# The late steps of a fused decoder layer: where one row update, two normalizations and the block transposes stand in VectorE's order

## The reference, cut to what matters

```
x = layernorm(x + attention1(x))                       # bf16, conv + 16 heads
x = layernorm(x + self_and_cross_attention(x, ctx))    # fp32, 16 heads, causal self part (512 keys)
                                                       # plus cross part (1024 keys), softmax over keys
x = layernorm(x + routed_ffn(x))                       # cluster and tile choice, spline; layernorm with
x = layernorm(x)                                       # gamma and beta, then a last plain layernorm
```

## Time and profile before

| | us |
|---|---|
| median of 3 runs | 2223.72 (2222.45 to 2225.03) |
| the profiled execution, its own time | 2221.05 |
| its span, first to last instruction | 2219.3 |
| PE busy | 2093.4 (94%) |
| DVE busy | 1754.5 (79%) |
| ACT busy | 1533.8 (69%) |
| POOL busy | 755.5 (34%) |

### The profile page before, as it was taken

The page is one execution under the profiler, slowest core; times in us unless marked ns, Lnnn a source line. Parts: engine busy times, 40 slices in busy tenths (PEclk is TensorE's granted clock), DMA queues, the critical chain, the costliest instruction groups (busy, mean ns, idle before and its releaser), DMA issues.

```text
span 2219.3 us, 39450 instructions
## 1 busy us (share of the span) xinstructions
PE 2093.4 (94%) x13138; PEld 911.5 (41%) x13138; DVE 1754.5 (79%) x4869; ACT 1533.8 (69%) x3361; POOL 755.5 (34%) x802
## 2 busy tenths in 40 slices
PE   5999999999999999999999999999999999989983
PEld 2344334543444434543335433454344533444332
DVE  6957779688987889778897788968888787977754
ACT  2936887478865888458894688747886578846861
POOL 3026521165113650155402653116521353004620
PEclk8899999999999999999999999999999999999995
DMA  3700034000520006100160003400043000610000
GB/s 111 138 10 1 1 67 86 11 2 1 114 49 10 2 20 124 20 11 2 39 124 10 1 1 76 87 11 1 1 96 58 11 1 11 113 30 1 1 11 10
DMA packets 250858, 81.80 MB, mean 37 GB/s; under 512 B 236064, under 2 KB 247328, under 8 KB 250656
## 3 DMA queue, kind: packets, MB, share of 16 engines
q1 hardware_dynamic: 250656, 79.29, 17.6%
HBM read 16.35 MB, written 4.19 MB: 9 GB/s over the span
## 4 chain that ended last, share of the span: by engine, by line
PE 76%; DVE 12%; ACT 8%; issue 3%; DMA 1%; SPq 0%; POOL 0%; DVEq 0%; POOLq 0%; ACTq 0%
PE bank L1738 14%; PE bank L1807 14%; PE bank L1798 10%; PE bank L1421 7%; PE bank L1734 6%; ACT work L772 5%; PE bank L1795 4%; PE bank L1691 4%; DVE work L977 3%; PE bank L1554 3%; PE bank L1541 2%; PE bank L1577 2%; PE bank L1848 2%; PE bank L1767 1%; DVE stats L982 1%
## 5 line engine op out<-in xcount | busy, mean ns | idle before, releaser
L831 ACT ACTIVATE work<-bank 128x512 f32<-128x512 f32 (+3 forms) x1536 | 723.0, 549 | 261.9 <-PE bank L1795 140.5
L1244 DVE TENSOR_REDUCE top_half<-bank 128x1 f32<-128x512 f32 x1024 | 636.4, 683 | 139.7 <-PE bank L1738 138.4
L1738 PE MATMUL bank<-k_c,q_c 32*128 32x512 f32 x2048 | 536.0, 618 | 0.0
L1798 PE MATMUL bank<-q_c,k_c 32*128 32x512 f32 x2048 | 467.4, 624 | 7.4 <-DVE q_c L1270 6.0
L772 ACT ACTIVATE work<-work,neg 128x512 bf16<-128x512 bf16 x512 | 362.7, 716 | 30.6 <-DVE work L977 29.8
L1807 PE MATMUL bank<-work,v_flat 128*32 128x512 f32 (+3 forms) x3072 | 365.0, 551 | 0.6 <-ACT work L831 0.3
L977 DVE TENSOR_SCALAR_CACHE_REDUCE work<-bank 128x512 bf16<-128x512 f32 x512 | 322.3, 685 | 35.2 <-PE bank L1523 25.1
L1241 DVE CUSTOM_DVE_ANT_0 masked<-bank,mask_w 128x384 bf16<-128x384 f32 (+3 forms) x512 | 226.6, 489 | 118.5 <-PE bank L1734 113.9
L654 POOL TENSOR_TENSOR featA<-featA,featB 128x512 f32<-128x512 f32 (+3 forms) x232 | 241.9, 1043 | 225.9 <-ACT featB L844 223.0
L1738 PEld LDWEIGHTS bank<-k_c,q_c 32*128 32x128 f32 x2048 | 210.9, 183 | 159.8 <-DVE top_half L1244 125.7
L615 POOL TENSOR_SCALAR ln_r<-mv 128x4 f32<-128x4 f32 x32 | 9.0, 281 | 748.9 <-DVE mv L986 748.9
(11 more groups left out here) (208 smaller groups left out, 2627.6 us busy)
## 6 DMA issues: line engine op xcount, KB each, us to landing
xT_pad<-xT SPq DMA_DIRECT2D x16, 256.0 KB, 2.9
ctx_sb<-ctxT SPq DMA_DIRECT2D x8, 512.0 KB, 3.4
x_res<-x SPq DMA_DIRECT2D x8, 512.0 KB, 5.0
out<-r_sb SPq DMA_DIRECT2D x8, 512.0 KB, 2.9
work<-work SPq DMA_TRANSPOSE x112, 4.5
qk_sb<-qkT SPq DMA_DIRECT2D x1, 512.0 KB, 4.6
pe_sb<-pe_w SPq DMA_DIRECT2D x1, 256.0 KB, 4.0
v_sb<-vT SPq DMA_DIRECT2D x1, 256.0 KB, 5.0
```

The source lines that it names most:

```text
L831: nc.scalar.activation(pT[:, s % PT_SLOTS, g, q0:S], exp_bank(n)[:, 0:S - q0], ACT.Exp, scale=SCALE).then_inc(pT_ready, 1)
L1244: nc.vector.tensor_reduce(top_half[:, i % 2, g, u // 2, u % 2:u % 2 + 1], scores, AX.X, ALU.max, negate=True).then_inc(slot_out, 1)
L1738: mm(dst, q_c[rows, i, P * t:P * (t + 1)], k_c[rows, i, S * half:S * (half + 1)], start=True, stop=True, tile_position=(GW * g, 0)).then_i ...
L1798: mm(dst, k_c[rows, i, P * u:P * (u + 1)], q_c[rows, i, :], start=True, stop=True, tile_position=(GW * g, 0)).then_inc(sT_mm, 1)
```

## The change

Three edits in DVE's order and one in a wait of PE:

```diff
-    QK_LATE = {LATE_STEP + 2: (0,), LATE_STEP + 4: (1,), LATE_STEP + 6: (2,), LATE_STEP + 8: (3,)}
+    QK_LATE = {LATE_STEP + 4: (0,), LATE_STEP + 5: (1,), LATE_STEP + 6: (2,), LATE_STEP + 7: (3,)}
...
                 for s in range(ALL_STEPS):
-                    if prev and s == LATE_STEP:
-                        third_sums(c, sf)
-                    if prev and s == LATE_STEP + 2:
+                    if prev and s == LATE_STEP + 4:
                         third_norm(c)
-                    if prev and s == LATE_STEP + 5:
+                    if prev and s == LATE_STEP + 6:
                         last_sums(c, sf)
-                    if prev and s == LATE_STEP + 7:
+                    if prev and s == LATE_STEP + 8:
                         last_norm(c)
...
                     for part in end_rows(s) if s >= LATE_STEP else []:
                         put_rows(*part)
+                    if prev and s == LATE_STEP:
+                        third_sums(c, sf)
...
                     if n >= FIRST_LATE + len(LATE_EXP_BANKS):
                         pe.wait_ge(pT_ready, b * ALL_SCORES + n - len(LATE_EXP_BANKS) + 1)
-                    elif n >= FIRST_LATE + 2:
-                        pe.wait_ge(slot_out, base + uses["late"])
+                    elif n >= FIRST_LATE + LATE_RING:
+                        at = LATE_EXP_BANKS[n - FIRST_LATE]
+                        pe.wait_ge(slot_out, base + max(use for use in range(uses["late"]) if use % RING == at) + 1)
```

## The result

| | before | changed |
|---|---|---|
| median of 20 runs each, us | 2224.57 (2220.91 to 2235.14) | 2215.11 (2209.24 to 2225.31) |
| ratio, 95% interval | | 0.9948 [0.9937, 0.9960] |
| profiled execution, us | 2221.05 | 2210.52 |
| mean granted clock of PE, profiled execution | 0.972 | 0.976 |

A forecast was written before the change was run, and what follows sets the result against it. PE held 76% of the chain and stopped 0.85 us at step 40 for DVE's `put_rows`. Rows first 6.4 us less POOL 0.5 gave 5.9 off 2223.72, 2217.8 us; the range for 8 in 10 was 2212.5 to 2222.3.

The forecast's parts named there:

- What bounds the kernel, and rows first: PE at step 40 waits for `put_rows` behind `third_sums`; moving it first gains 0.92 us in seven batches, 6.4 us.
- What becomes late on DVE: DVE's late steps: output copy at most 0.1 us late, at +9.4; `third_norm` from +10.0; 3.52 us to spare at the end.
- The moves of `third_norm` and of the transposes: On DVE: `third_norm` ends 4.5 us later; transposes are done by +19.8, PE needs them at about +23.8, costing nothing.
- POOL: Later convolution and rstd delay `last_norm` to +24.2, meeting the next scores: 0.1 us lost in five batches, 0.5 us.
- the lower bound: POOL term's bound of 0: the bias addition, beside which L630 took 1.80 us instead of 1.57, now comes before it.
- the control: The first batch, with no previous batch to normalize: step 40 at +4.72, next batch's first score tile at +24.21.
- Rival 1: POOL's chain through `last_norm` ends after the next batch's first scores: 0.5 us in five batches, 2219.8 us; chance 0.13.
- Behind POOL's second half: SP's loads end at +31.9, the first DMA block transpose is wanted at +32.04: fits with 0.1 us to spare.
- Bank waits: PE's transposed scores 154 and 155: 154 may start 0.62 us earlier, 155 waits as before; costed at 0.
- The clock: PE's low-clock stretch costs a batch 2.4 us; shifting batches can change how many have it, either way.
- rival 3: PE's clock turns in favour: one or two batches lose the low stretch, 2215.4 or 2213.0 us; chance 0.13.
- The sum: Whole kernel: 6.4 - 0.5 = 5.9 us off, giving 2215.1 profiled and 2217.8 for the median.

The follow-up runs named there:

- rows_behind_sums: The changed kernel with `third_sums` again ahead of `put_rows`: median 2229.88 us, 1.0015 of before.
- fill4: The changed kernel with four needless matmuls on PE ahead of step 40's transposed scores, in seven batches: median 2226.23 us, 0.9996 of before.
- transposes_as_before: The changed kernel with the four pairs of block transposes back at steps 40, 42, 44 and 46: median 2243.02 us, 1.0066 of before.
- changed_again: The changed kernel run once more, unaltered, on another occasion: median 2216.16 us, 0.9946 of before.
- no_bank_waits: The changed kernel with the old wait of PE for the banks: median 2219.37 us, 0.9971 of before.
- rows_only: The kernel before with only `put_rows` moved ahead of `third_sums`: median 2250.15 us, 1.0096 of before.
- late_bank_last_on_before: The kernel before with the new bank waits and late bank order 4, 5, 2, 3, 0, 1: median 2233.32 us, 1.0026 of before.

## Why the prediction was right, point by point

- *What bounds the kernel, and rows first.* Right. `put_rows` at +2.76 and step 40 at +4.72 in all seven batches; the first tile at +24.29 instead of +25.13, 0.84 us each. rows_behind_sums and fill4 show that this is the place that pays.
- *What becomes late on DVE.* Right to 0.1 us: the copy at +9.43 against +9.4, `third_norm` from +10.04, `finish` at +14.22, the last copy at +19.69. But that "its reader on PE comes later still" passed over how little later, 0.2 us. The moves of `third_norm` and of the transposes were costed at nothing, as if the gain didn't hang on them; the experiments show that they are what makes rows first pay at all.
- *POOL.* Half right. The term of 0.5 us is 0 as a POOL effect: `last_norm` ended at +23.7 or earlier, and not at +24.2: the chain took 9.65 us and not 10.12. Of these 0.47 us, 0.24 are L630, which the bias addition no longer met (1.56 and not 1.80), as the lower bound had it, and 0.24 are L615 (0.24 and not 0.48), which no term had. In its place stands a term that I didn't have: the first tile came 0.08 us later than the control's +24.21 in every batch, also in the seventh, where DVE was idle for 2.67 us before it. In rows_behind_sums it is 0.08 too (25.21 against 25.13). So it isn't a wait for POOL. PE's first scores (L1523) start at +23.78 in both, and DVE takes the first tile out 0.42 us later in the control and 0.51 later in the changed kernel. In all kernels run here it is 0.42 to 0.43 where a block transpose or the output copy stands just ahead of that tile on DVE, and 0.51 to 0.52 where `last_norm` does. So it comes with making `last_norm` the last thing ahead of the tile. In sum 0.08 x 6 = 0.5 us, the same as the forecast's term by accident. Rival 1 did not occur here; its mechanism is real, as transposes_as_before shows, at 1.26 us a batch.
- *Behind POOL's second half.* Right: the first block transpose by DMA went out at 570.45, +32.11, against a wanted +32.04. But the second batch gave 0.7 us back later, when PE waited 1.05 us for one such transpose (at 629.79), and its distance to the third shrank by only 0.11. The wait comes back at this place, 0.89 in changed_again and 0.97 in no_bank_waits, and was 0.42 before. "A transposed tile late by a few tenths costs nothing" is therefore not borne out in this batch; what makes the wait longer stays open.
- *Bank waits.* Right, 0, by the reason given. What was missed is the edit beside it: the wait per bank is worth 1.2 us a batch once the banks are taken in the order in which they come free.
- *The clock.* The term that was mis-sized. The forecast put it at 0 and its favourable turn in rival 3; measured are 3.9 us of gain from it, together with the forecast's mechanism. The distance from the third to the fourth batch fell from 265.70 to 262.41 us, with the clock at 1.00 where it had been 0.50. That is the luck of one execution: in changed_again the fourth and the sixth batch have the clock at 0.50 at nearly the same distances behind L1248 (+86 and +124) as the third of before. Its price was read wrong too: that batch of before has a second such stretch, from 925.4 to 928.8, so the 2.4 us are those of two, some 1.2 us each. And all three runs that the forecast started from were by chance better than before's usual ones: 2223.72 against 2226.64 over 76.
- *The sum.* 5.9 forecast; 6 x 0.84 = 5.0 by the first tiles of the third to eighth batch, and 0.93 in the last late steps, together 6.0; 7.3 (error 0.4) at equal clock; 10.5 between the two profiled executions, of which 0.004 x 1500 = 6 is the clock's. The traces don't place all of the 7.3: in the three batches that are free of the lower clock in both profiles, the distance from one L1248 to the next shrank by 0.11, 0.52 and 1.14 us (second, fourth, sixth), 0.6 in the mean where the first tile had gained 0.84. So 5.9 is right as the size of the mechanism; the rest of the 9.5 between the medians is mostly the clock's and was not foreseen.

## What to carry to other kernels

When a stop is taken from the critical engine, reckon anew what everything behind it has to spare, since the stop gave each other producer its slack: here DVE had stood idle for 0.63 us ahead of one output copy, afterwards it didn't, the copy's reader followed with 0.2 us to spare, and both moves that looked idle were needed to keep even that. Where a ring is split anew, hand out its slots in the order in which they come free, and look whether another engine holds the chain behind them first. A new stop can cost more than its own length, as the lower clock behind it in rows_only shows. And compare kernels at equal granted clock, as soon as single runs of one kernel spread by more than the effect that is sought, but first look in the trace whether the edit itself has brought the lower clock, since then it belongs to the edit.

## What the runs showed of the hardware

- `last_norm` has four instructions of 0.40 us each where POOL is at rest, 1.36 us for the four. Where POOL's L626 runs beside it (560.04 and 559.99 us, second batch) the four take 2.04, and two of them 0.79 and 0.69. In the seventh batch of the changed kernel, where POOL is at rest, DVE:

```profile
1872.65 1.36 DVE L991 TENSOR_SCALAR r_sb<-r_sb,mv,ln_r 128x256 f32<-128x256 f32 x4
1876.67 0.69 DVE L977 TENSOR_SCALAR_CACHE_REDUCE work<-bank 128x512 bf16<-128x512 f32 x1 [2.67 <-PE bank L1523]
```

  The Trainium skill's "SBUF — State Buffer", section "SBUF: two separate sides", says that GpSimd and certain VectorE instructions (in a 2-port mode, or with two inputs in SBUF) hold their shared ports for a whole instruction, the other blocking fully. No row tells whether `last_norm`'s instructions are of that kind. Here the meeting costs DVE 0.7 us in all, while L626 itself takes 1.62 instead of 1.57: DVE isn't blocked for L626's length.
- The first tile's 0.08 to 0.09 us behind `last_norm` instead of a transpose or a copy, although DVE had been idle for 2.67 us in between (seventh batch). No run tells its cause.
- A stop of PE can be followed by the lower clock: behind the one of 2.62 us in rows_only the clock fell to 0.50 in five batches of six, behind the one of 2.05 us in late_bank_last_on_before in one of seven, behind the one of 0.85 us in before in none of seven. In no other profile does it stand at 0.50 within 25 us behind L1248 in any batch.
- From the end of an output copy on DVE to the start of the matmuls on PE that wait for it, 0.15 us went by in each of the three kernels where this wait was the last.
- One kernel's time moves by 16 us with the mean granted clock (0.975 to 0.966).
